# A graph kernel on one core: in-degrees from the sorted destinations, and the edge rows fetched in another block

## Chip, cores and metric

One core of one Trainium2 chip runs the whole kernel in one launch. The metric is the device time in microseconds. The engines are PE (TensorE; PEld is its weight load), DVE (VectorE), ACT (ScalarE), POOL (GpSimd) and SP (SyncE, which here only issues DMAs).

## What is computed

A stack of four graph layers on 3125 nodes with 16 features. The graph has 50000 random undirected edges, each in both directions, and a self-loop for each node: 103125 edges, sorted by destination. Each layer is x = x + layer(relu(layernorm(x))). Cut to what matters here:

```python
edge_index = stack([src, dst])                        # dst is sorted, 103125 edges, loops included
# layer 0, three GCN layers; adds its own self-loops once more
deg = segment_sum(ones, col);  norm = rsqrt(deg)[row] * rsqrt(deg)[col]
h = relu(agg(norm * (h @ W1)[row]) + b1); h = relu(agg(norm * (h @ W2)[row]) + b2); agg(norm * (h @ W3)[row]) + b3
# layer 1: messages of the sources summed per destination, between dense layers of 256
# layer 2: agg of x[src] * out_deg[src]**-0.5, times in_deg**-0.5 (degrees at least 1)
# layer 3: per edge, softmax over the in-edges of a destination, 16 x 16 channels:
e1 = (efeat @ W_msg + b_msg).reshape(E, 16, 16) * feat[src][:, :, None]
e2 = (efeat @ W_attn + b_attn).reshape(E, 16, 16) * feat[src][:, :, None]
ft = segment_sum(e1 * softmax_over_segment(e2, dst), dst).sum(axis=1)
```

## The kernel before

The kernel is a row of blocks. All five engines have a program in a block, and the next block begins when all of them are through, so nothing overlaps from one block to the next. The first blocks are these.

`build_edges`, first block (L203 to L318), the preparation. The edge table `edges` is a dense matrix of edge counts, sources in tiles of 128 partitions (25 tiles), destinations in 3136 columns, in bfloat16. It is built in strips of 16 destination columns from groups of 256 sorted edges; a "pair" is one group with one strip. The preparation finds group and strip of each of 600 pairs from the last destination of each of 403 groups (`cuts`, `below`, `gidx`; L243 to L288), clears the table (POOL 12 tiles, L236; DVE 13 tiles, L289), writes the diagonal (L298), gathers sources and destinations of the pairs with ten indirect DMAs on POOL (L231), and turns them into `qT` and `loT` (L301 to L318).

`build_edges`, second block (L324 to L377), the edge loop: 15 turns of 40 pairs. For a pair DVE makes two one-hot tiles `q_hot` (L337) and, for each five pairs, one `lo_hot` (L333); PE multiplies them and adds the strip as it stands (L358, L362); ACT copies the sum back into the strip (L375). POOL and SP have nothing to do.

`degrees` (L380 to L432): `times_edges` (L639) multiplies a matrix of ones with the whole table, 175 matmuls; the column sums are turned by 50 small matmuls (L406) into `indeg` and `deg`. SP loads `x` there.

`edge_groups` (L478 to L614) sorts the edges of each node into groups of at most four (`SLOTS`). It computes from `indeg` the first edge of each of 28160 groups (`start`) and which of the four slots are empty (`missing`). Its histogram is a product of one-hot tiles, 25 of each kind (L577 to L579, L532). It writes `start_wide` to memory, waits for that, loads it again one group further on into `q_following` (L612), and compares (L597, L599).

`Fetch` (L435 to L475) fetches the rows of edge features in the order of the groups. A turn is an index copy on POOL (L451) and four gathers of 128 rows of 512 bytes (L456) into `got0` or `got1`, and SP stores the tile to `edges_order` (L469). There are 56 turns, in pairs; a turn waits until the tile of two turns ago has been gathered and stored. 46 turns run beside `layer0`, the other ten beside `layer1_nodes`, two in each of its five rounds.

`layer0` (L650 to L809) runs `times_edges` three times on PE (the second with two groups of weights, 350 matmuls, L645), with ACT taking each chunk out (L712), small products (L728, L738, L745, L749, L756) and DVE work in between. `layer1_nodes` (L812 to L951) runs the dense layers of layer 1 over five parts. `layer1_sum` (L954) is the first reader of `edges_order`. After that come `layer1_post`, `layer2` and the attention with its own 880 gathers (L1481).

Waits: `Line.then` and `Steps.then` let an engine wait for its own instruction; other waits are counts of semaphores.

## Time and profile before

| what | us |
|---|---|
| median of 3 runs (lowest, highest) | 3127.6 (3121.86, 3134.39) |
| span of the profiled execution | 3126.8 |
| PE, DVE, ACT, POOL busy | 2351.3, 2224.5, 1698.7, 1398.1 |
| preparation, 0 to 66.2 | 66.2 |
| edge loop, 66.2 to 470.3 | 404.1 |
| degree pass, 470.3 to 516.4 | 46.1 |
| edge groups, 516.4 to 551.0 | 34.6 |
| layer 0, 551.0 to 879.3 | 328.3 |
| nodes of layer 1, 879.3 to 1005.0 | 125.7 |

The profile is one execution, whose span agrees with the median of the runs. "Busy" counts instructions in work; "idle before" is the time an engine stood still ahead of an instruction, with what ended it, and "issue" there means that the profile shows nothing it waited for. "remote" is a releaser that the records don't name. A row of windows gives the stretch, its length, then busy us and (x instructions) of PE, PEld, DVE, ACT and POOL (or of those engines that a filter leaves), the granted clock, the DMA share and GB/s. A row of the page's part 5 gives count, busy us, mean ns of one, and the idle time before them. PEclk is the clock granted to TensorE as a share of 2.4 GHz. Ends of matmuls are modelled, and instructions on POOL are recorded roughly.

### The profile page before, as it was taken

The page shows a single profiled execution, that of the slowest core. Times are in us where ns is not written, and L with a number is a line of the kernel's source. Part 1 is how long each engine was busy: PE and PEld are TensorE (multiplying, and loading weights), DVE is VectorE, ACT ScalarE, POOL GpSimd, SP SyncE. Part 2 cuts the span into 40 slices and gives each one's busy share as a digit, 9 for nine tenths or more (in the row PEclk, how much of TensorE's full clock was granted, in tenths as well). Part 3 has the DMA queues.
Part 4 walks back from the last instruction along what each step waited for, and adds up shares of the span by engine and source line. Part 5 has one row for each costly group of instructions (what it writes and reads, how often), then busy time and mean ns, then how long its engine had stood idle before and what let it go on. Part 6 is the DMA issues. An engine that isn't in the chain of part 4 may idle for free. (4 is left out here: it accounts for less than half of the span.)

```text
span 3126.8 us, 38694 instructions
## 1 busy us (share of the span) xinstructions
PE 2351.3 (75%) x8098; PEld 1032.6 (33%) x8099; DVE 2224.5 (71%) x3656; ACT 1698.7 (54%) x6693; POOL 1398.1 (45%) x1220
## 2 busy tenths in 40 slices
PE   1888887656675998854788888888888888888840
PEld 1444443232453555331232223322232222322220
...
GB/s 17 0 0 0 0 0 6 85 87 88 52 62 171 150 149 146 73 19 17 64 67 72 63 80 67 63 72 76 70 65 72 63 80 67 63 72 68 70 47 89
DMA packets 122372, 201.38 MB, mean 64 GB/s; under 512 B 55271, under 2 KB 76664, under 8 KB 116448
## 3 DMA queue, kind: packets, MB, share of 16 engines
q1 hardware_dynamic: 84320, 170.52, 15.6%
...
q14 instruction: 21, 0.17, 0.0%
...
## 5 line engine op out<-in xcount | busy, mean ns | idle before, releaser
L1481 POOL DMA_INDIRECT hs<-h_table,gix x880 | 1103.8, 1254 | 451.2 <-issue 271.5
L1574 ACT ACTIVATE e<-wps,hs 128x32 f32<-128x32 f32 x5632 | 1029.8, 402 | 235.2 <-PE wps L1505 142.3
L1505 PE MATMUL wps<-w_edge,ef 18*128 18x512 f32 x1760 | 577.6, 707 | 316.1 <-ACT e L1574 135.1
L1527 PE MATMUL slot_sums<-e,ident 128*128 128x512 f32 x1408 | 761.3, 691 | 9.7 <-DVE e L1676 7.0
L1527 PEld LDWEIGHTS slot_sums<-e,ident 128*128 128x128 f32 x1408 | 296.6, 222 | 493.3 <-issue 464.3
L1505 PEld LDWEIGHTS wps<-w_edge,ef 18*128 18x128 f32 x1760 | 159.1, 200 | 691.5 <-ACT e L1574 274.8
L358 PE MATMUL acc<-q_hot,lo_hot 128*128 128x400 bf16 x1200 | 306.0, 337 | 48.7 <-DVE q_hot L337 46.8
L1611 DVE TENSOR_TENSOR e<-wps,hs 128x2048 f32<-128x2048 f32 x132 | 301.9, 2287 | 41.1 <-PE wps L1505 34.0
L375 ACT CAST edges<-acc 128x400 f32 x600 | 293.5, 492 | 59.0 <-PE acc L362 32.5
L337 DVE TENSOR_SCALAR q_hot<-qcol,qT 128x400 bf16<-128x400 bf16 x1200 | 293.9, 322 | 9.7 <-PE acc L362 9.5
L456 POOL DMA_INDIRECT got<-in_edge_rows,ix x224 | 224.9, 1004 | 100.7 <-issue 92.7
L645 PE MATMUL acc<-edges,parts 128*128 x875 | 201.6, 382 | 80.9 <-issue 31.9
L1658 DVE TENSOR_TENSOR e<-e,shifts 128x1024 f32<-128x1024 f32 x220 | 256.7, 1218 | 0.0
L1584 ACT ACTIVATE e<-e 128x1024 f32<-128x1024 f32 x220 | 241.7, 1108 | 26.4 <-issue 11.0
L1676 DVE TENSOR_TENSOR e<-e 128x1024 f32<-128x1024 f32 x220 | 253.5, 1220 | 0.0
L1035 PE MATMUL acc<-edges,msg_parts 128*128 (+1 forms) x1050 | 210.3, 355 | 25.3 <-DMA msg_parts<-msg 25.3
L362 PE MATMUL acc<-edges,ident_b 128*128 x600 | 202.9, 338 | 17.2 <-ACT edges L375 17.2
L514 POOL IOTA q_laneI<- 128x256 int32 x1 | 0.3, 341 | 470.7 <-ACTq L511 470.7
L712 ACT ACTIVATE agg<-acc 48x448 f32<-48x448 f32 (+1 forms) x21 | 11.3, 539 | 300.4 <-PE acc L645 148.1
L779 DVE TENSOR_TENSOR y<-small,deg 128x512 f32<-128x512 f32 (+1 forms) x8 | 4.6, 575 | 217.7 <-remote 204.8
L358 PEld LDWEIGHTS acc<-q_hot,lo_hot 128*128 128x128 bf16 x1200 | 130.5, 140 | 82.8 <-DVE q_hot L337 59.9
L645 PEld LDWEIGHTS acc<-edges,parts 128*128 128x128 bf16 x875 | 87.8, 103 | 192.7 <-issue 132.0
...
## 6 DMA issues: line engine op xcount, KB each, us to landing
...
hs<-h_table,gix POOLq DMA_INDIRECT x880
...
```

What stands on the lines that cost most here:

```text
L337: ins = nc.vector.tensor_scalar(q_hot[:, k % HOTS, s, :], qcol[:, :], qT[:, s, at], None, ALU.is_equal)
L358: nc.tensor.matmul(total, lo_hot[:, k // HOTS % 2, :, k % HOTS * 2 + s], q_hot[:, k % HOTS, s, :], start=(s == 0), stop=False)
L375: nc.scalar.copy(edges[:, :, bass.ds(s16, W)], acc[:, k % BANKS, 0:QW].rearrange("p (t w) -> p t w", w=W)).then_inc(taken, 1)
L645: ins = nc.tensor.matmul(out[:, bass.ds(n, 1), 0:CW], lhs(k), edges[:, k, bass.ds(n * CW, CW)], start=(g == 0 and k == 0), stop=(g == last ...
L1481: nc.gpsimd.indirect_dma_start(out=hs[u][:, s, :], out_offset=None, in_=d["h_table"], in_offset=bass.IndirectOffsetOnAxis(ap=gix[u][:, s:s ...
L1505: nc.tensor.matmul(wps[:, bank, :], ef[u][k:k + KM, g * P:(g + 1) * P], w[k:k + KM, :], start=True, stop=True).then_inc(a_mult, 1)
L1527: ins = nc.tensor.matmul(sums[:, g % 2, :], ident[:, :], e[u][:, g * SLOTS + c, :], start=(c == 0), stop=(c == SLOTS - 1))
L1574: ins = nc.scalar.mul(e[u][:, s, at], wps[:, bank, at], hs[u][:, s, f:f + 1])
L1584: nc.scalar.activation(e2, e2, ACT.Exp).then_inc(a_exp, 1)
L1611: nc.vector.tensor_tensor(e[u][:, s0:s1, :].rearrange("p s (i c) -> p (s i) c", c=2 * F), wps[:, 0:s1 - s0, :].rearrange("p s (i c) -> p ( ...
L1658: nc.vector.tensor_tensor(e2, e2, bc(shift(u, g), 1, SLOTS), ALU.subtract).then_inc(a_sub, 1)
L1676: ins = nc.vector.tensor_tensor(pair[:, :, 1, :], pair[:, :, 0, :], pair[:, :, 1, :], ALU.mult)
```

## The change

`degrees` is gone. The preparation becomes `prepare_pairs`, then comes `edge_groups`, then `fill_edges` (the edge loop). All edge rows are fetched in `fill_edges`; `layer0` and `layer1_nodes` lose the fetch.

- In-degrees: for each of 3125 nodes ACT counts in which group of 256 sorted destinations the first edge of this node lies (`coarse`, one activation with an accumulated output for each tile of 128 nodes), POOL gathers these groups of `dst` (25 indirect DMAs, two sets of five), and ACT counts inside them (`fine`). The rank of the next node (two small matmuls, `later` and `corner`) minus a node's own is its in-degree.
- Compare and reduction of the pair search become one DVE instruction with an accumulated output.
- POOL clears ten tiles of the table ahead of the gathers, DVE eight and three; the last four tiles hold the tiles of the preparation (`lent`) and are cleared on POOL in `edge_groups`, where ACT writes their part of the diagonal.
- `edge_groups` computes also the square roots and reciprocals for `deg`, keeps the one-hot tiles in a ring of ten (a wait of DVE for PE), and leaves the load of `q_following` and the computation of `missing` to `fill_edges`.

```diff
+LENT = 4
...
-            build_edges(nc, io, keep, d, sem)
-            degrees(nc, io, keep, d, sem)
-            with nc.sbuf_tensor("start", [P, GORDER], I32) as keep["start"]:
-                with ExitStack() as fetching:
-                    fetch = Fetch(nc, fetching, io, keep, d, sem)
-                    edge_groups(nc, io, keep, d, sem)
-                    layer0(nc, io, keep, d, sem, fetch)
-                    layer1_nodes(nc, io, keep, d, sem, fetch)
+            with ExitStack() as building:
+                pairs = pair_tiles(nc, building)
+                prepare_pairs(nc, io, keep, d, sem, pairs)
+                edge_groups(nc, io, keep, d, sem, pairs)
+                fill_edges(nc, io, keep, d, sem, pairs, Fetch(nc, building, io, pairs, d, sem))
+            layer0(nc, io, keep, d, sem)
+            layer1_nodes(nc, io, keep, d, sem)
             layer1_sum(nc, io, keep, d, sem)
...
+    loT, qT, lane, qcol, strip, ident_b = (pairs[n] for n in ("loT", "qT", "lane", "qcol", "strip", "ident_b"))
+    BLANK = TILES * 10 // 25
+    MORE = BLANK + TILES * 8 // 25
...
+                nc.gpsimd.affine_select(out=ident[:, :], in_=ident[:, :], compare_op=ALU.not_equal, fill=1.0,
+                                        base=0, pattern=[[-1, P]], channel_multiplier=1).then_inc(b_consts, 1)
+                nc.gpsimd.affine_select(out=later[:, :], in_=later[:, :], compare_op=ALU.not_equal, fill=1.0,
+                                        base=-1, pattern=[[-1, P]], channel_multiplier=1)
+                nc.gpsimd.affine_select(out=corner[:, :], in_=corner[:, :], compare_op=ALU.not_equal, fill=1.0,
+                                        base=P - 1, pattern=[[-1, P]], channel_multiplier=1).then_inc(b_consts, 1)
+                nc.gpsimd.memset(edges[:, 0:BLANK, :].rearrange("p t c -> p (t c)").bitcast(I32), 0
+                                 ).then_inc(b_blank, 1)
+                pool.wait_ge(b_pairs, 1)
+                for k in range(PAIR_TILES):
+                    for rows_of, name in ((srcg, "src"), (dstg, "dst")):
+                        nc.gpsimd.indirect_dma_start(
+                            out=rows_of[:, k, :], out_offset=None,
+                            in_=io[name].rearrange("(g e) -> g e", e=GROUP),
+                            in_offset=bass.IndirectOffsetOnAxis(ap=gidxI[:, k:k + 1], axis=0),
+                        ).then_inc(b_gather, 16)
+                pool.wait_ge(b_groups, 1)
+                for t in range(TILES):
+                    r = t // SET
+                    if r >= 2 and t % SET == 0:
+                        pool.wait_ge(b_fine, (r - 1) * SET)
+                    nc.gpsimd.indirect_dma_start(
+                        out=rows[:, r % 2, t % SET, :], out_offset=None,
+                        in_=io["dst"].rearrange("(g e) -> g e", e=GROUP),
+                        in_offset=bass.IndirectOffsetOnAxis(ap=coarseI[:, t:t + 1], axis=0),
+                    ).then_inc(b_rows[r % 2], 16)
+
...
+                    ins.then_inc(b_pe, 1)
+                pe.wait_ge(b_rank, 1)
+                nc.tensor.matmul(after[:, :], later[:, :], rank[:, 0:TILES], start=True, stop=False)
+                nc.tensor.matmul(after[:, :], corner[:, :], rank[:, 1:TILES + 1], start=False, stop=True
+                                 ).then_inc(b_after, 1)
...
+                act.wait_ge(b_node, 1)
+                act.wait_ge(b_last, 1)
+                for t in range(TILES):
+                    if t >= 2:
+                        act.wait_ge(b_coarse, t - 1)
+                    nc.scalar.activation(sign[:, t % 2, :], last[:, :], ACT.Sign, bias=half_less[:, t:t + 1],
+                                         accum_out=coarse[:, t:t + 1]).then_inc(b_coarse, 1)
+                act.wait_ge(b_coarse, TILES)
+                for t in range(TILES):
+                    r = t // SET
+                    if t % SET == 0:
+                        act.wait_ge(b_rows[r % 2], 16 * SET * (r // 2 + 1))
+                    if t >= 2:
+                        act.wait_ge(b_fine, t - 1)
+                    nc.scalar.activation(sign[:, t % 2, 0:GROUP], rows[:, r % 2, t % SET, :], ACT.Sign,
+                                         bias=half_less[:, t:t + 1], accum_out=fine[:, t:t + 1]).then_inc(b_fine, 1)
+
...
+                v.add(nc.vector.tensor_copy(qcol[:, :], qcolI[:, :]))
+                dve.wait_ge(b_pe, 1)
+                for k in range(PAIR_TILES):
+                    v.then(nc.vector.tensor_scalar(below[:, :], cuts[:, :], pair[:, k:k + 1], 0.0, ALU.is_le, ALU.add,
+                                                   accum_out=gidx[:, k:k + 1]))
+                v.then(nc.vector.tensor_scalar(below[:, :], cuts[:, :], float(RUN), 0.0, ALU.is_le, ALU.add,
+                                               accum_out=middle[:, :]))
+                v.then(nc.vector.tensor_scalar(middle[:, :], middle[:, :], -1.0, float(RUN), ALU.mult, ALU.add))
...
+                nc.vector.tensor_scalar(first[:, :], first[:, :], float(W), None, ALU.mult).then_inc(b_pairs, 1)
+                v.add(nc.vector.memset(edges[:, BLANK:MORE, :], 0.0))
+
+                dve.wait_ge(b_coarse, TILES)
+                v.then(nc.vector.tensor_scalar(coarse[:, :], coarse[:, :], -0.5, 0.5 * GROUPS, ALU.mult, ALU.add))
+                v.then(nc.vector.tensor_scalar(coarse[:, :], coarse[:, :], float(GROUPS - 1), None, ALU.min))
+                nc.vector.tensor_copy(coarseI[:, :], coarse[:, :]).then_inc(b_groups, 1)
+                v.add(nc.vector.memset(rank[:, TILES:TILES + 1], float(EPAD)))
+                v.add(nc.vector.memset(edges[:, MORE:TILES - LENT, :], 0.0))
...
+                for t in range(TILES - LENT):
+                    w = min(P, COLS - t * P)
+                    v.add(nc.vector.tensor_copy(edges[:, t, t * P:t * P + w], ident[:, 0:w]))
...
+                v.then(nc.vector.tensor_scalar(fine[:, :], fine[:, :], -0.5, 0.5 * GROUP, ALU.mult, ALU.add))
+                nc.vector.scalar_tensor_tensor(rank[:, 0:TILES], coarse[:, :], float(GROUP), fine[:, :],
+                                               ALU.mult, ALU.add).then_inc(b_rank, 1)
+                dve.wait_ge(b_rank, 1)
+                dve.wait_ge(b_after, 1)
+                v.then(nc.vector.tensor_tensor(indeg[:, :], after[:, :], rank[:, 0:TILES], ALU.subtract))
+
+
...
+def fill_edges(nc, io, keep, d, sem, pairs, fetch):
...
+            @block.sync
+            def _(sp):
+                sp.dma_start(following[:, :], d["start_wide"][1:GTOTAL + 1].rearrange("(p g) -> p g", p=P)
+                             ).then_inc(q_short, 16)
+                with sp.Fori(0, fetch.PAIRS) as i:
+                    for v in range(2):
+                        fetch.store(sp, i, v)
+                fetch.wait_stored(sp, fetch.PAIRS)
+
+            @block.gpsimd
+            def _(pool):
+                for v in range(2):
+                    fetch.gather(pool, 0, v)
+                with pool.Fori(1, fetch.PAIRS) as i:
+                    for v in range(2):
+                        fetch.gather_again(pool, i, v)
+
...
 
+                v = Line(dve, q_missing)
+                dve.wait_ge(q_short, 16)
+                v.then(nc.vector.tensor_tensor(following[:, :], following[:, :], run[:, 1, :], ALU.subtract))
+                for c in range(1, SLOTS):
+                    v.then(nc.vector.tensor_scalar(missing[:, 0:GSTEPS, c], following[:, :], float(c), None, ALU.is_le))
                 dve.wait_ge(taken, RUNS + TURNS * BODY)
...
-def degrees(nc, io, keep, d, sem):
...
+def edge_groups(nc, io, keep, d, sem, pairs):
...
+                nc.gpsimd.memset(edges[:, TILES - LENT:TILES, :].rearrange("p t c -> p (t c)").bitcast(I32), 0
+                                 ).then_inc(q_blank, 1)
 
...
+                v.then(nc.vector.tensor_scalar(raw[:, 1, :], indeg[:, :], 1.0, None, ALU.max))
+                nc.vector.tensor_scalar(raw[:, 0, :], indeg[:, :], 1.0, 1.0, ALU.add, ALU.max).then_inc(q_raw, 1)
...
+                    nc.vector.tensor_scalar(lo_hot[:, at, 0, :], lane[:, 0:GSTEPS], lo[:, t:t + 1], None, ALU.is_equal)
+                    nc.vector.tensor_scalar(lo_hot[:, at, 1, :], lane[:, 0:GSTEPS], lo[:, t:t + 1], short[:, t:t + 1],
                                             ALU.is_equal, ALU.mult).then_inc(q_hot, 1)
-                dve.wait_ge(q_hist, 1)
+                v.wait_all()
+                dve.wait_ge(q_sqrt, 1)
+                v.add(nc.vector.reciprocal(deg[:, 0, :], raw[:, 0, :]))
+                v.add(nc.vector.reciprocal(deg[:, 2, :], raw[:, 1, :]))
+                dve.wait_ge(q_hist, TILES)
                 for a in range(2):
                     v.then(nc.vector.tensor_tensor_scan(run[:, a, :], zero[:, :], hist[:, a, :], 0.0,
                                                         ALU.add, ALU.add))
...
+                dve.wait_ge(q_done, 1)
+
+            @block.scalar
+            def _(act):
+                act.wait_ge(q_raw, 1)
+                nc.scalar.activation(raw[:, :, :], raw[:, :, :], ACT.Sqrt).then_inc(q_sqrt, 1)
+                act.wait_ge(q_blank, 1)
+                for t in range(TILES - LENT, TILES):
+                    w = min(P, COLS - t * P)
+                    ins = nc.scalar.copy(edges[:, t, t * P:t * P + w], ident[:, 0:w])
+                ins.then_inc(q_loops, 1)
+                act.wait_ge(q_sqrt, 1)
+                act.wait_ge(q_loops, 1)
...
                              ).then_inc(q_out, 16)
                 sp.wait_ge(q_out, 80)
-                sp.dma_start(following[:, :], d["start_wide"][1:GTOTAL + 1].rearrange("(p g) -> p g", p=P)
-                             ).then_inc(q_out, 16)
-                sp.wait_ge(q_out, 96)
...
-def layer0(nc, io, keep, d, sem, fetch):
+def layer0(nc, io, keep, d, sem):
...
                                  ).then_inc(c_w, 16)
-                with sp.Fori(0, FETCH0) as i:
-                    for v in range(2):
-                        fetch.store(sp, i, v)
                 sp.wait_ge(c_w, 16 * 12)
-                fetch.wait_stored(sp, FETCH0)
-
-            @block.gpsimd
-            def _(pool):
-                for v in range(2):
-                    fetch.gather(pool, 0, v)
-                with pool.Fori(1, FETCH0) as i:
-                    for v in range(2):
-                        fetch.gather_again(pool, i, v)
 
...
-def layer1_nodes(nc, io, keep, d, sem, fetch):
+def layer1_nodes(nc, io, keep, d, sem):
...
                                      parts[:, :, :, f * P:(f + 1) * P]).then_inc(n_dm, 16)
-                    for v in range(2):
-                        fetch.store(sp, FETCH0 + c, v)
                 sp.wait_ge(n_dh, 16 * ROUNDS)
                 sp.wait_ge(n_dm, 32 * ROUNDS)
-                fetch.wait_stored(sp, fetch.PAIRS)
-
-            @block.gpsimd
-            def _(pool):
-                for c in range(ROUNDS):
-                    for v in range(2):
-                        fetch.gather_again(pool, FETCH0 + c, v)
 
```

## Rows read from the trace of the kernel before

**Rows 1.** Windows of the first five stages and of the attention.
```profile
0.00:66.20 66.20, 6.24 (x22) 4.64 (x23) 47.65 (x81) 0.02 (x1) 27.99 (x22) 1.00 0.17 20
66.20:470.30 404.10, 336.93 (x1800) 188.21 (x1800) 375.94 (x1322) 312.78 (x615) 0.00 (x0) 1.00 0.00 0
470.30:516.40 46.10, 42.85 (x225) 25.43 (x225) 5.59 (x15) 1.53 (x2) 0.00 (x0) 0.89 0.05 5
516.40:551.00 34.60, 15.33 (x31) 4.04 (x31) 25.14 (x114) 0.00 (x0) 1.57 (x8) 0.50 0.03 10
551.00:879.30 328.30, 216.42 (x925) 114.66 (x925) 42.64 (x70) 11.54 (x22) 189.07 (x229) 0.74 0.27 74
...
1388.00:2950.00 1562.00, 1269.69 (x3072) 438.30 (x3072) 1410.12 (x1572) 1267.18 (x5825) 1103.76 (x880) 0.80 0.22 66
```

**Rows 2.** Timeline of the preparation: start us, us, engine, instruction, [idle before].
```profile
7.57 0.64 DVE L271 TENSOR_SCALAR below<-cuts,pair 128x403 f32<-128x403 f32 x1 [1.80 <-PE cuts L243]
8.24 0.57 DVE L272 TENSOR_REDUCE gidx<-below 128x1 f32<-128x403 f32 x1
...
17.20 0.17 DVE L288 TENSOR_SCALAR first<-first 128x5 f32<-128x5 f32 x1
...
21.58 17.13 DVE L289 MEMSET edges<- 128x20488 uint32 x1 [4.21 <-issue]
...
29.07 0.94 POOL L231 DMA_INDIRECT dstg<-in_dst,gidxI  x1 [0.30 <-issue]
30.01 15.88 POOL L236 MEMSET edges<- 128x18912 int32 x1
```

**Rows 3.** The page's part 5, ACT's copy out of PSUM in the edge loop.
```profile
L375 ACT CAST edges<-acc 128x400 f32 x600 | 293.5, 492 | 59.0 <-PE acc L362 32.5
```

**Rows 4.** Timeline at the end of the edge groups, SP's queue.
```profile
546.17 0.35 SPq L612 DMA_DIRECT2D q_following<-start_wide  x1
```

**Rows 5.** Windows of L645 alone, layer 0's three passes.
```profile
561.90:636.50 74.60, 49.61 (x175) 17.86 (x175) 0.75 0.34 91
668.00:778.30 110.30, 80.66 (x350) 34.38 (x350) 0.89 0.32 87
832.60:868.60 36.00, 35.75 (x175) 17.76 (x175) 0.93 0.00 0
```

**Rows 6.** Timeline behind the first pass, PE and DVE.
```profile
636.87 3.64 PE L728 MATMUL small<-w,agg 48*128 48x64 f32 x16 [9.55 <-issue]
...
643.50 0.69 DVE L779 TENSOR_TENSOR y<-small,deg 128x512 f32<-128x512 f32 x1 [81.92 <-remote]
```

**Rows 7.** The page's part 5, all gathers of edge rows on POOL.
```profile
L456 POOL DMA_INDIRECT got<-in_edge_rows,ix x224 | 224.9, 1004 | 100.7 <-issue 92.7
```

**Rows 8.** Timeline, POOL beside DVE, layer 0 and layer 1's nodes.
```profile
650.51 0.97 POOL L456 DMA_INDIRECT got<-in_edge_rows,ix  x1 [0.81 <-issue]
650.59 0.43 DVE L783 TENSOR_SCALAR y<-y 128x512 f32<-128x512 f32 x1
...
884.63 5.10 DVE L933 TENSOR_TENSOR edges<-edges,ident 128x128 bf16<-128x128 bf16 x25
...
885.77 0.22 POOL L451 COPY ix<-start 128x4 int32<-128x4 int32 x1
886.80 3.77 POOL L456 DMA_INDIRECT got<-in_edge_rows,ix  x1 [0.81 <-issue]
```

**Rows 9.** Timeline of DVE in the edge loop, one stretch of five pairs.
```profile
104.58 0.82 DVE L333 TENSOR_TENSOR lo_hot<-lane,loT 128x1280 bf16<-128x1280 bf16 x1
105.31 2.42 DVE L337 TENSOR_SCALAR q_hot<-qcol,qT 128x400 bf16<-128x400 bf16 x10
```

**Rows 10.** Windows of L1574 alone (ACT), attention's start and later.
```profile
1419.30:1442.40 23.10, 4.88 (x17) 0.50 0.07 6
...
1580.00:1700.00 120.00, 81.87 (x438) 0.82 0.24 73
```

381 lines of the change are left out of this document (172 added, 209 removed).

## The prediction, made before the changed kernel was run

> **What bounds the kernel now.** Read first by stage. The chain of work that ended last is of no help: it covers only the last steps. The windows [rows 1] are of more use: the code is a row of blocks that wait for one another, so each block's length is its own critical path, and what leaves a block leaves the time. The first five are the preparation of the pairs (66.2 us), the edge loop (404.1), the degree pass (46.1), the edge groups (34.6) and layer 0 (328.3); the nodes of layer 1 follow. Nothing behind those is changed, and no edge row is read before they end. In the edge loop DVE is busy 376 of 404 us and POOL not at all; in layer 0 it is the other way round. The second view is L645, the product with the edge table, pass by pass [rows 5]. The third pass of layer 0, with no fetch beside it, took 36.0 us for 175 matmuls. The first, with gathers beside it, took 74.6 us for the same 175, and the second 110.3 for 350. So the fetch is not free where it stands. The third view is the gathers on POOL and what DVE does to them [rows 7, 8].
>
> **Part 1: no degree pass, another way to the in-degrees.** Old way, three blocks ahead of layer 0 besides the loop: 66.2 + 46.1 + 34.6 = 146.9 us [rows 1]. The 46.1 go whole. In their place the preparation grows. DVE: six pairs of compare (0.64) and reduction (0.57) [rows 2] become six single instructions of about 0.67, so the pair indices come some 3.5 us earlier than 17.4, less about 1.2 for the node numbers and the ends: near 15. ACT: 25 activations over 403 columns, not in the trace; the nearest row is 0.49 for 400 columns out of PSUM [rows 3], and I take 0.6 for the accumulated output (bounds 0.49 to 0.8). From about 7 us they end near 22 (19 to 27), under DVE's clearing of eight tiles (8/13 of 17.1 us [rows 2], to 26); they cost nothing while that lasts. POOL is the path. Its clearing of ten tiles is 10/12 of 15.9 us = 13.2, now ahead of the gathers, so it ends near 17.5; then come ten gathers every 1.25 us (0.94 and a gap of 0.30 [rows 2]), to 30; then 25 new gathers of dst rows, 25 x 1.25 = 31.3, to 61. Beside them DVE runs its copies and its casts of 1280 columns, which hold gathers up (part 4): 0 to 12 us, I take 5. Landing, the last five activations, the two small matmuls and the subtraction: 5 to 10, I take 8. Sum 74 (66 to 83). DVE's own way (to 26, three tiles more 4, then what now lies between the end of POOL's clearing, 30.0 + 15.9, and 66.2, copies and casts, 20) ends near 50 and is hidden. The edge groups lose their tail, since the load of q_following is issued at 546.2, where 80 counts of q_out are there [rows 4], and the block ends at 551.0: 34.6 - 4.8 + 0.7 for two reciprocals = 30.5. Its ring of ten hot tiles asks DVE to wait for PE five tiles back, and PE kept up (bounds 0 and 2). The clearing of the four lent tiles (5.3 us on POOL) and four copies on ACT lie beside some 30 us of DVE work. New: 74 + 30.5 = 104.5. Change **-42** (-52 to -32).
>
> **Part 2: layer 0 without the fetch.** First pass 74.6 - 36.0 = 38.6; second 110.3 - 2 x 36.0 = 38.3 [rows 5]. Behind the first pass DVE starts on a finished small product 3.0 us late [rows 6]: 636.9 + 3.6 = 640.5, start 643.5. Together **-80**. The third pass begins at a lower clock, so twice its length is rather long for the second, and I take 87 as the upper bound; the lower is 0, if the stalls have another cause (a rival). The clock does not make the difference: it was 0.75 and 0.89 in the slow passes and 0.93 in the quiet one [rows 5], and there are gaps in which PE had nothing issued. SP's queue in that block loses 46 stores; the weight loads ahead of them are unchanged.
>
> **Part 3: nodes of layer 1.** Rounds there are a chain over PE, ACT and DVE; the last edge store only ends the block beside the last message stores. **-1** (-3 to 0).
>
> **Part 4: the fetch beside the edge loop.** Unhindered it is 224.9 + 100.7 = 325.6 us of POOL [rows 7], against 404.1 us of loop, so there are 78 us to spare. What does DVE's stream do to it? If the gather gets in at the next instruction's end, the mean wait is 3/4 x 0.12 + 1/4 x 0.41 = 0.19 us; 224 gathers and 56 index copies make 53 us. 326 + 53 = 379 < 404: hidden, with 25 us left. The bounds are 0 and, if it is starved through whole stretches, +148 (rival A). I take the fair case, because the index copy beside the same stream took 0.22 us, so a stream as such does not shut POOL out, and because DVE idles 28 us in the loop, where any gather gets in. The stores on SP have no queue behind them that anybody waits for; `missing` is computed behind the loop, where DVE waits for ACT's last copy: +2 (0 to 3). If the loop should become shorter than 379 us, this cover is gone and each microsecond of the rest is paid in full.
>
> Here the Trainium skill speaks against the change. Its page "SBUF — State Buffer", section "Who interferes with whom", says that a VectorE instruction in a two-port mode holds the port pair it shares with GpSimd for its whole length, and that descriptors of a DMA issued by GpSimd can't be written meanwhile. The 0.97 us gather with the fast tensor_scalar inside it does not agree for the part behind the start; the held-up gather agrees for the start.
>
> **Sum.** The profiled execution: 3126.8 (its span; the median of the runs is 3127.6, so the two are the same for this). 3126.8 - 42 - 80 - 1 + 2 = **3005 us**.
>
> **Rivals.**
> A. DVE starves the gathers. By the strict form a gather moves on only outside q_hot, that is 0.89 of every 3.31 us, so one gather in 3.3: 404/3.3 = 122 of 224 are done at the loop's end, and 102 x 1.45 (325.6/224) = 148 us stand bare: 3153. If one in three waits about 3 us, as one of the POOL instructions in the stream of 25 did, the mean is 2.7 us, 150 are done, 74 x 1.45 = 107: 3112. For: DVE works 93% of the loop, its instructions overlap. Against: the gather with the fast instruction inside. The page above would give the strict form.
> B. Slower: the stall moves along. With gathers at full pace PE had one matmul in 0.43 us in the first pass instead of 0.21 (74.6 and 36.0 over 175), and ACT, at the start of the attention, 17 short activations in 23.1 us, 1.36 us each, where later it had 438 in 120 [rows 10]. The loop needs one activation and three matmuls for a pair in 404.1/600 = 0.67 us. At 1.36 us a pair the 326 us of fetch cover 240 pairs, the other 360 take 242: the loop becomes 568, +164, and 3005 + 164 = **3169**. It decides (slower than 3142) from a mean of 1.16 us a pair during the fetch. For: it was seen twice. Against: both times DVE was idle, and in the attention as a whole, with DVE busy 1410 of 1562 us and 880 gathers on POOL [rows 1], ACT's pace is whole; in the loop DVE is busy and breaks up the gathers' rhythm. Once DVE waits for a stalled PE, though, it no longer breaks it up, so the state could hold itself.
> C. The change doesn't bring what it says in layer 0: the stalls of L645 belong to the code and not to the gathers. 3005 + 80 = 3085. Against: the same function ran the third pass and the degree pass (46.1 us with everything) without them.
>
> **Chances.** Forecast (2982 to 3035) 0.52; A 0.24 (3035 to 3153, likeliest 3112); B 0.17 (3090 to 3180, likeliest 3169); C 0.07. 0.5% is 15.6 us, about what a measurement of this kernel can tell from no change. Slower by more needs over 3142: most of B and a quarter of A, 0.18. Within: between 3111 and 3142, less what lies below: 0.06. Faster 0.76. Range 2982 to 3145: it leaves out B's upper part, a bit of A, and a preparation better than reckoned.
>
> **What would show it.** Right: L231's successor gathers end near 61 us, the block near 74, the loop starts near 105; the loop's block is 404 to 410 us, with POOL's last gather before its end and L337's successor at 0.24 us each; the three passes of layer 0 at 36, 70 and 36 us, that block at 248. A: POOL gathers far beyond 1 us while DVE keeps its pace, and a stretch behind the loop with POOL alone. B: PE and ACT idle for "issue" in the loop, POOL at 0.94, and the loop quick again once the fetch ends. C: passes unchanged with POOL empty. Wrong altogether if the 25 rank gathers are slowed so that the preparation passes 90 us.

## The result, and the profile after

The changed kernel took 3185.7 us (median of four runs), the kernel before 3126.5 beside it: a ratio of 1.0188 (1.0154 to 1.0223), slower by 1.9% where 3.9% less was forecast. The profiled execution has a span of 3170.7 us. It can be read by stages like [rows 1]. The windows of the changed kernel, with the columns of [rows 1], in order the preparation, the edge groups, the edge loop with the fetch, and layer 0:

```profile
0.00:85.80 85.80, 8.60 (x28) 6.18 (x29) 55.63 (x87) 28.71 (x102) 56.16 (x52) 0.90 0.26 56
85.80:120.40 34.60, 15.34 (x31) 4.04 (x31) 29.21 (x114) 2.26 (x6) 6.70 (x8) 0.50 0.02 7
120.40:689.00 568.60, 402.26 (x1800) 201.38 (x1800) 392.70 (x1325) 292.97 (x600) 239.37 (x280) 0.81 0.19 52
689.00:925.50 236.50, 185.58 (x925) 111.12 (x925) 42.61 (x71) 11.56 (x22) 0.00 (x0) 0.79 0.00 1
```

| stage | before | forecast | after |
|---|---|---|---|
| preparation | 66.2 | 74 | 85.8 |
| degree pass | 46.1 | 0 | 0 |
| edge groups | 34.6 | 30.5 | 34.6 |
| edge loop | 404.1 | 406.1 | 568.6 |
| layer 0 | 328.3 | 248.3 | 236.5 |
| all behind it | 2247.5 | 2246.5 | 2245.2 |
| span | 3126.8 | 3005 | 3170.7 |

The degree pass, layer 0 and all behind it came out as forecast or better. The preparation and the edge groups together are 15.9 us over the forecast (120.4 against 104.5). The loss is the edge loop, +164.5 us. Three groups of the changed kernel, answering to [rows 3] and [rows 7] (busy time, mean ns, then the idle time before them and what ended it):

```profile
L505 ACT CAST edges<-acc 128x400 f32 x600 | 293.0, 493 | 300.0 <-PE acc L492 137.3 <-remote 98.3 <-issue 45.9
L462 DVE TENSOR_SCALAR q_hot<-qcol,qT 128x400 bf16<-128x400 bf16 x1200 | 307.4, 327 | 113.3 <-remote 60.7 <-PE acc L492 45.5 <-issue 6.9
L531 POOL DMA_INDIRECT got<-in_edge_rows,ix x224 | 227.4, 1015 | 98.4 <-issue 96.4 <-POOL ix L526 1.6 <-DMA edges_order<-got 0.3
```

The gathers are as quick as in [rows 7] (1015 ns, 98.4 us of gaps): DVE did not starve them. ACT does its 600 copies in the old time for each, but idles 300 us around them (30 of these ahead of the first). 98 us end with "remote" and some with "issue", for which the profile shows no releaser in the kernel. I read the waits for PE as the same stall seen from behind PE; the profile doesn't show that by itself. Windows of L505 alone, the first while the fetch runs and the second behind it:

```profile
121.00:463.00 342.00, 120.15 (x249) 0.69 0.32 86
463.00:687.00 224.00, 172.82 (x351) 1.00 0.00 1
```

That is 342/249 = 1.37 us a pair beside the gathers and 224/351 = 0.64 behind them. Rival B had said 1.36 us a pair and a loop of 568 us. The 1.37 is a mean over an uneven stretch: between 250 and 300 us there were 25 copies, between 300 and 350 us 60.

### The profile page after: what moved, and what is told of

Same layout as the page of the kernel before. It is cut to its first block and busy times, and to the rows that moved or that the text cites. A ratio compares the mean times of both kernels' runs of the same rounds, so it can differ in the third digit from the quotient of the medians.

```text
span 3170.7 us, 38247 instructions
## 1 busy us (share of the span) xinstructions
PE 2347.7 (74%) x7879; PEld 1019.1 (32%) x7880; DVE 2247.7 (71%) x3651; ACT 1712.2 (54%) x6783; POOL 1434.8 (45%) x1251
## 5 line engine op out<-in xcount | busy, mean ns | idle before, releaser
L505 ACT CAST edges<-acc 128x400 f32 x600 | 293.0, 493 | 300.0 <-PE acc L492 137.3
L462 DVE TENSOR_SCALAR q_hot<-qcol,qT 128x400 bf16<-128x400 bf16 x1200 | 307.4, 327 | 113.3 <-remote 60.7
L488 PE MATMUL acc<-q_hot,lo_hot 128*128 128x400 bf16 x1200 | 346.3, 374 | 54.1 <-DVE q_hot L462 47.1
L492 PE MATMUL acc<-edges,ident_b 128*128 x600 | 223.2, 372 | 115.3 <-issue 78.7
L531 POOL DMA_INDIRECT got<-in_edge_rows,ix x224 | 227.4, 1015 | 98.4 <-issue 96.4
L737 PE MATMUL acc<-edges,parts 128*128 x875 | 174.1, 364 | 40.5 <-DVE mean L849 13.5
L488 PEld LDWEIGHTS acc<-q_hot,lo_hot 128*128 128x128 bf16 x1200 | 141.1, 143 | 104.5 <-DVE q_hot L462 59.9
L1702 DVE TENSOR_TENSOR pairs<-e 128x1536 f32<-128x1536 f32 x88 | 131.0, 1489 | 30.0 <-ACT e L1645 30.0
L1133 ACT COPY efT<-tr 128x512 f32<-128x512 f32 x56 | 32.8, 586 | 215.7 <-PE tr L1115 215.7
L492 PEld LDWEIGHTS acc<-edges,ident_b 128*128 128x128 bf16 x600 | 60.3, 100 | 265.5 <-issue 261.7
```

What stands on the lines that cost most here:

```text
L462: ins = nc.vector.tensor_scalar(q_hot[:, k % HOTS, s, :], qcol[:, :], qT[:, s, at], None, ALU.is_equal)
L488: nc.tensor.matmul(total, lo_hot[:, k // HOTS % 2, :, k % HOTS * 2 + s], q_hot[:, k % HOTS, s, :], start=(s == 0), stop=False)
L492: nc.tensor.matmul(total, ident_b[:, :], edges[:, :, bass.ds(s16, W)], start=False, stop=True).then_inc(multiplied, 1)
L505: nc.scalar.copy(edges[:, :, bass.ds(s16, W)], acc[:, k % BANKS, 0:QW].rearrange("p (t w) -> p t w", w=W)).then_inc(taken, 1)
```

## A condition that comes and goes

All experiments were measured on other occasions, and the kernel before was quicker on all of them, by nearly 4% on five of eight. This has to be told first, since every reading depends on it. The first line is the measurement of the result; each other line is one session, all on one chip. Numbers with a star come from a single run:

| kernel before, us | with it (ratio to it) |
|---|---|
| 3126.5 | the changed kernel 1.0188 |
| 3011.7 | e1 0.985, e2 0.997\*, e3 0.976, e4 0.969\* |
| 3009.1 | the changed kernel (e5) 0.979, the kernel before again (e6) 1.001\*, e7 0.975 |
| 3008.1 | e8 0.969 |
| 3012.7, chip A | e9 1.006\*, e10 0.9945 |
| 3068.5\* | e11 1.011\* |
| 3073.2, chip A | e12 0.983, e13 0.9825 |
| 3118.1, chip A | the changed kernel (e14) 1.0134, e15 0.990 |
| 3011.1 | e16 0.967, e18 0.993, e17 0.9685 |

I call some 3010 us the quiet condition and anything above 3060 the stalled one. Chip A had both, so it is no fixed property of a chip. Nothing in the kernels differs between them. A ratio is only ever taken within one session.

The two conditions also differ in what the traces hold, and this bears on every reading below. A trace records the updates of semaphores. All thirteen traces of the quiet condition hold 30.5 to 31.2 thousand such records, all seven of the stalled one (before, after, e11 to e15) 19.0 to 20.8 thousand, with the same number of instructions in the same kernel. The missing ones lie where gathers run: of the landings of DMAs, before and e6 (the same kernel, quiet) have 173 and 180 in the preparation, but 1222 and 3864 in layer 0 and 8704 and 15736 in the attention. Beside the edge loop the 224 gathers should leave 3584 records of landing and the 56 stores 896. e5 (the changed kernel, quiet) has 3498 and 878 of them, the profile of the result 776 and 187. So a wait that ends with "remote" or "issue" in a stalled stretch may only lack the record of its releaser, and these words don't say what the engines waited for. And as every time here is that of an execution with such a record, no run shows whether the stall is there without the recording.

## Experiments

**The fetch alone put back** (e1: the in-degrees stay new, the fetch goes back into layer 0, 46 turns, and the nodes of layer 1, ten; the expectation calls the 46 "pairs of turns", they are turns).

```diff
-                fill_edges(nc, io, keep, d, sem, pairs, Fetch(nc, building, io, pairs, d, sem))
-            layer0(nc, io, keep, d, sem)
...
+                fill_edges(nc, io, keep, d, sem, pairs)
+            layer0(nc, io, keep, d, sem, fetch)
...
```

> The changed kernel with the fetch alone put back where it was (46 pairs of turns in layer 0, five in the nodes of layer 1); the new in-degrees stay. It splits the two halves of the change. Theory: the edge loop's 570 us are all due to the fetch beside it and layer 0's gain is all due to the fetch leaving. Then the fill is back at 404 to 408 us, layer 0 at 328, the preparation and edge groups stay at 85.4 and 34.9, and the time is 3126.8 + 19.2 - 46.1 + 0.3 = 3100 us (3095 to 3110). Rival (the fill is slow through something else that the change moved, such as the memory in which the pair tiles now lie or the missing counts behind the loop): the fill stays above 450 us and the time above 3150.

Measured: 2966.9 us, a ratio of 0.9854 (0.9838 to 0.9871). Windows of the loop and of layer 0:

```profile
119.00:508.00 389.00, 338.20 (x1800) 188.89 (x1800) 373.80 (x1325) 295.42 (x600) 0.18 (x1) 1.00 0.00 0
508.00:787.00 279.00, 186.51 (x925) 111.35 (x925) 43.59 (x72) 11.56 (x22) 191.30 (x230) 0.75 0.31 87
```

The loop without the fetch is not 404 but 389 us: 15 us that nothing in the forecast explains (e10 does). Layer 0 with its 46 turns of the fetch is 279 us, not 328. In the quiet condition the fetch in layer 0 does not stall PE (e6 below has the passes); POOL's own length bounds the block.

**Gathers first, stores behind** (e2). SP's stores wait for all gathers, and POOL no longer waits for stores, so what is stored are the rows of the last turns.

```diff
+                for v in range(2):
+                    sp.wait_ge(fetch.gathered[v], 16 * TURN * fetch.PAIRS)
...
-        pool.wait_ge(self.stored[v], i * 16)
```

> In the changed kernel all 224 gathers run first, each turn waiting for the gathers only, and all 56 stores follow when they are done, still beside the edge loop; so the rows stored are those of the last turns, and the edge features are not the reference's. It tells gathers from stores. Theory G, the software gathers stall PE, ACT and DVE: a pair takes about 1.4 us while POOL gathers (some 330 us, 235 pairs) and 0.65 us beside the stores, fill some 560 to 570 us. Theory S, the stores' traffic on SP does it: 0.67 us a pair while POOL gathers, over 1 us beside the stores, fill some 430 to 480 us.

Neither theory was tested: in the quiet condition the loop took 394.5 us with the gathers beside it, 0.66 us a pair. (The gathers and stores then ran some 79 us past the loop.)

**Paced gathers** (e3), each turn waiting for ten pairs more.

```diff
+                        pool.wait_ge(taken, i * 20 + 10 * v)
```

> The changed kernel with each turn of four gathers also waiting until ACT has taken out ten pairs more, so that 56 turns spread over 560 of the 600 pairs. A turn takes POOL about 6.0 us, ten pairs 6.5 to 6.7. Theory U, the stall needs some 20 us of unbroken gathers and a pause of POOL of about 2 us ends it: as soon as pairs slow down POOL waits, so the stall can't hold itself; fill 405 to 460 us, time 3010 to 3065. Theory V, the stall is there from the first gathers on and lasts as long as they are issued: in each turn 6.0 us pass at 1.4 us a pair, the other 6 pairs take 4 us, 10 us a turn, fill about 570 us and the time as the changed kernel's, 3160 to 3190.

Measured: 2934.1 us, 0.976 (0.973 to 0.979), fill 397.9 us. There was no stall to be held off, so theories U and V stay undecided. It says that a fetch stretched over the whole loop costs 9 us above the bare 389.

**ACT clears in POOL's place** (e4), in the preparation and in the edge groups. DVE's 21 copies of the diagonal also move behind its transposed copies.

```diff
-                nc.gpsimd.memset(edges[:, 0:BLANK, :].rearrange("p t c -> p (t c)").bitcast(I32), 0
-                                 ).then_inc(b_blank, 1)
+                for t in range(BLANK):          # on ACT, behind the 25 coarse activations
+                    words = edges[:, t, :].bitcast(F32)
+                    nc.scalar.copy(words, nought[:, 0:1].broadcast_to(list(words.shape))).then_inc(b_blank, 1)
...
```

> The changed kernel with POOL's two clearings (10 tiles in the preparation, 4 in the edge groups) done by ACT as copies of a zero, the 21 diagonal copies on DVE moved behind the transposed copies. Theory L: POOL's clearing shuts out DVE's small instructions for its whole length (13.4 us of DVE L334 in the preparation, 5.4 us of DVE L627 in the edge groups, both ending with a POOL memset). Then both are under 0.3 us, the pair indices are ready near 15 us instead of 27, the ten gathers end near 28, the preparation is 72 to 80 us instead of 85.4 and the edge groups 29 to 31 instead of 34.9. Rival W, these instructions wait for something else: they stay long, the preparation stays over 83 us.

Lines of the changed kernel's timeline, the preparation and the edge groups (start, length):

```profile
3.56 13.36 DVE L334 CAST own<-turnI 128x5 f32<-128x5 int32 x1
3.66 13.23 POOL L265 MEMSET edges<- 128x15760 int32 x1
...
87.22 5.35 POOL L599 MEMSET edges<- 128x6304 int32 x1
87.23 5.38 DVE L627 TENSOR_SCALAR raw<-indeg 128x25 f32<-128x25 f32 x1
```

The same two DVE instructions in e4's, and its windows of the two stages:

```profile
3.58 0.18 DVE L337 CAST own<-turnI 128x5 f32<-128x5 int32 x1
...
71.19 0.17 DVE L628 TENSOR_SCALAR raw<-indeg 128x25 f32<-128x25 f32 x1
```

```profile
0.00:69.80 69.80, 7.88 (x28) 5.63 (x29) 42.54 (x87) 42.75 (x112) 40.11 (x52) 0.86 0.32 69
69.80:100.30 30.50, 15.32 (x31) 4.03 (x31) 24.09 (x114) 7.98 (x10) 1.57 (x8) 0.50 0.02 8
```

Theory L holds. A cast of five columns on DVE took 13.36 us while POOL was clearing, and 0.18 us without that. The preparation went to 69.8 us (82.6 in e5, the changed kernel in the same condition), even below the 72 expected, the groups from 34.7 to 30.5, the forecast's own number. How much of the preparation's 12.8 us is due to the moved diagonal copies isn't separated; the two DVE instructions alone give 13.2 and 5.2.

**The changed kernel and the kernel before again** (e5 and e6, both unaltered).

> The changed kernel itself, unaltered, beside the kernel before, timed again and with a profile of its own. In the experiments so far the kernel before took 3011.7 us instead of 3126.5, and no run stalled beside gathers, so this asks whether the stall belongs to the kernel or to where it ran. If the kernel before is at about 3012 again: the changed kernel has no stalls either, its edge loop is about 395 to 408 us and its time that of the quick-preparation kernel (2919) plus 16 + 5 = 2935 to 2945, a ratio of 0.975 to 0.978. If the kernel before is at about 3127: the changed kernel is at 3172 to 3200 with a loop of 567 us, a ratio of 1.015 to 1.022. A mixture, such as 3012 beside 3180, would make the stall a thing of the changed kernel alone.

> The kernel before, unaltered, for a profile beside the others. If it is at about 3012: the passes of the product with the edge table in layer 0 are about 36, 70 and 36 us instead of 74.6, 110.3 and 36.0, though the fetch is beside them, layer 0 is bound by POOL's gathers and takes 280 us instead of 328, the edge loop is still 404 us with 15 loads of ACT's table, one in each turn of 40 pairs, and the other 65 us are in the attention. If it is at about 3127, all is as in the profile shown.

In the same session 2940.5 against 3009.1 us, a ratio of 0.979 (0.975 to 0.983): the changed kernel is 2.1% faster in the quiet condition and 1.3 to 1.9% slower in the stalled one. First e5's windows of loop and layer 0, and two groups of it; then e6's window of layer 0:

```profile
117.30:528.00 410.70, 344.23 (x1800) 191.58 (x1800) 383.75 (x1325) 295.22 (x600) 301.91 (x280) 0.97 0.27 72
528.00:764.50 236.50, 185.82 (x925) 112.29 (x925) 42.44 (x70) 11.54 (x22) 0.00 (x0) 0.79 0.00 1
```

```profile
L505 ACT CAST edges<-acc 128x400 f32 x600 | 295.2, 492 | 130.3 <-PE acc L492 105.1
L531 POOL DMA_INDIRECT got<-in_edge_rows,ix x224 | 284.9, 1272 | 98.2 <-issue 50.6 <-POOL ix L526 45.2 <-DMA edges_order<-got 2.4
```

```profile
551.00:832.00 281.00, 185.53 (x925) 111.11 (x925) 43.12 (x71) 11.55 (x22) 191.28 (x230) 0.74 0.31 87
```

Of ACT's idle time 105.1 of 130.3 us end with PE now, and the gathers are slower instead: 1272 ns, since DVE keeps its pace. Layer 0 of the kernel before is 281.0 us where it was 328.3 [rows 1]. The rest of the difference of 118 us between the conditions is nearly all in the attention: from its start to the end of the span 1747.3 us in the profile shown and 1680.3 in e6, 67 us.

The quiet ledger, e6 to e5: preparation +16.4 (66.2 to 82.6), degree pass -45.7, groups -0.1, fill +6.4 (404.3 to 410.7), layer 0 -44.5 (281.0 to 236.5), the rest -3.0; together -70.5.

**Quick preparation with paced gathers** (e7), e3 and e4 together.

> The changed kernel with both trials together: ACT clears in POOL's place, and each turn of four gathers waits for ten more pairs. If the kernel before is at about 3012: preparation 66 to 70, edge groups 27, edge loop 398 with nothing behind it, 2926 - 18 = 2908 us (2903 to 2915), 0.966 of the kernel before. If it is at about 3127, theory U (the stall needs unbroken gathers) gives a loop of 405 to 460 us and a ratio of 0.96 to 0.98, theory V (the stall is there whenever gathers run) a loop of about 560 us and a ratio of 1.01.

Measured 2931.8 us (0.975), not 2908: this time the paced fetch ended late and the fill took 416 us. Pacing adds to the fetch's length what a turn loses when it starts late, and never gets it back.

**The last two of 28 fetch pairs in layer 0** (e8, and again as e17; both on e4's kernel).

```diff
+FETCH0 = GORDER // TURN // 2 - 2
...
-                with pool.Fori(1, fetch.PAIRS) as i:
+                with pool.Fori(1, FETCH0) as i:
...
```

> The quick-preparation kernel, with only 26 of the 28 pairs of fetch turns beside the edge loop and the last two pairs (16 gathers) at the start of layer 0, where POOL is idle. Where the kernel before takes 3010 us: the fetch of 28 pairs took 400 us beside a loop of 396 to 400 (gathers of 1.27 us instead of 1.00 beside DVE's stream) and the block ended 8 to 10 us behind the loop's last instruction; 26 pairs need 371 us, so the loop alone ends the block, 396 to 398 us, and layer 0 stays at 238: 2919 - 9 = 2910 us (2905 to 2916), 0.966 to 0.969 of the kernel before. Rival: the fetch slows the loop itself as much as before and layer 0 pays for the two pairs, then 2916 to 2925. Where the kernel before takes 3127 the stall is back: the ratio is 1.00 to 1.02.

> The split kernel without rests (26 pairs beside the loop, two in layer 0), a second time: 0.969 where the kernel before takes 3010; where it takes 3073 to 3127 the loop stalls as the changed kernel's, 480 to 560 us, and the ratio is that of the changed kernel less 0.010: 0.99 to 1.005. The long rests should beat it there by 0.01 to 0.02.

2915.7 us, 0.9694 (0.968 to 0.971), and 2912.9 us, 0.9685 (0.966 to 0.971). The fill is 395.6 us; without the split it was 406.7 (e4). The end of the fetch no longer sticks out behind the loop.

**What holds a gather up** (e9): q_hot's source at every other element, so that DVE leaves its fast form.

```diff
...
-                            ins = nc.vector.tensor_scalar(q_hot[:, k % HOTS, s, :], qcol[:, :], qT[:, s, at], None,
+                            ins = nc.vector.tensor_scalar(q_hot[:, k % HOTS, s, :], qcol[:, :, 0], qT[:, s, at], None,
```

> The changed kernel with the column numbers that DVE compares in the q_hot instructions held at every other element, so that these leave the two-times-fast form (0.24 us for 400 columns) and take about 0.42 us; it tells what holds up the gathers beside the loop (1.27 us mean beside it, 1.00 without; a tenth of them 2.7 us, as long as a run of ten q_hot). Theory P, fast instructions back to back keep the port from POOL: the gathers are at 1.0 us mean, none over 1.7, and all 224 end 340 us after the first, while the loop takes about 600 us. Rival Q, any DVE instruction does it: gathers of 4 us and more appear, mean 1.4 us or more. If the kernel before takes 3127 here, the stall is back and PE, ACT and DVE show it beside the gathers: then a loop with more slack (1.0 us a pair by DVE) still falls to 1.4 us a pair.

A stretch of e5's timeline, and then e9's groups:

```profile
299.88 2.77 POOL L531 DMA_INDIRECT got<-in_edge_rows,ix  x1 [0.30 <-issue]
300.11 2.41 DVE L462 TENSOR_SCALAR q_hot<-qcol,qT 128x400 bf16<-128x400 bf16 x10
...
302.95 1.13 POOL L531 DMA_INDIRECT got<-in_edge_rows,ix  x1 [0.30 <-issue]
```

```profile
L462 DVE TENSOR_SCALAR q_hot<-qcol,qT 128x400 bf16<-128x400 bf16 x1200 | 416.0, 426 | 0.0
...
L531 POOL DMA_INDIRECT got<-in_edge_rows,ix x224 | 236.3, 1055 | 98.3 <-issue 52.4 <-POOL ix L526 45.2 <-DMA edges_order<-got 0.6
```

In e5 a gather that meets the head of ten q_hot back to back ends 0.13 us behind the tenth; 23 of the 224 took over 2.5 us. In e9 DVE is busier (495.8 of 497.7 us of the block) and the gathers take 1055 ns, 223 of 224 under 1.13 us. So the fast form of these tensor_scalars holds the gathers up, not DVE's load; theory P. It is shown for tensor_scalar only: the stream in [rows 8] that held a gather for 3.77 us was of tensor_tensor. The loop's 600 us were wrong, it took 497.7: the slow form costs 0.35 us of busy time apiece.

**One ACT instruction ahead of the loop of the kernel before** (e10).

```diff
+                nc.scalar.copy(warm[:, :], ones[:, 0:1])
                 act.sem_inc(taken, RUNS)
```

> The kernel before with one copy of a 128x1 column on ACT ahead of the edge loop and nothing else. The profile of before has 15 loads of ACT's table, 1.28 us each, one in each turn of 40 pairs of the edge loop; the changed kernels have none there, and with no fetch beside it their loop took 388 us instead of 404. Theory M: the loads come because nothing on ACT ran ahead of the loop, and they cost the loop those 16 us. Then they are gone but one, the loop is 388 us, and the time is 16 us under the kernel before, a ratio of 0.9945 (0.993 to 0.996). Rival: the 16 us come from the shorter preparation or from where the pair tiles lie; then the loop stays at 404 and the ratio at 1.000.

ACT in the edge loop of the kernel before, a row that the forecast had not read, and then of e10:

```profile
L375 ACT ACT_TABLE_LOAD x15 | 19.2, 1283 | 96.9 <-PE acc L362 96.9
```

```profile
L368 ACT ACT_TABLE_LOAD x1 | 1.3, 1283 | 66.3 <-PEq L203 66.3
```

Ratio 0.9945 (0.9925 to 0.9966), loop 388.0 us instead of 404. With no ACT instruction ahead of the loop, its table is loaded anew in each of the 15 turns. The change got these 16 us as a side effect; its Sign activations on ACT stand ahead of the loop.

**Five kinds of fetch in one loop** (e11).

```diff
+                Q = fetch.PAIRS // 4              # POOL; a loop of Q pairs of turns for each kind
...
+                fetch.wait_stored(pool, Q)
+                with pool.Fori(Q, 2 * Q) as i:
+                    for v in range(2):
+                        pool.wait_ge(fetch.gathered[v], i * (16 * TURN))
+                        fetch.gather(pool, i, v)
+                fetch.wait_stored(pool, 2 * Q)
...
```

> The changed kernel with the fetch beside the edge loop cut into five stretches, so that one run tells what stalls PE and ACT, if anything does: (1) 14 turns of gathers with their stores, as in the changed kernel, (2) 14 turns of gathers with no store, (3) the 14 stores of these, one behind the other, POOL waiting (they store what the two buffers hold then, so these edge rows are not the reference's), (4) 14 turns with stores, POOL resting before every second turn until everything of the turn before has landed and is stored, some 5 us, (5) 14 turns as in (1). Where the kernel before takes about 3010 us, as in all experiments so far: 0.65 to 0.68 us a pair in all five, the fill 400 to 415 us. Where it takes about 3127: theory G (gathers stall the engines): about 1.4 us a pair in 1, 2 and 5, and 0.67 in 3; theory S (the stores' traffic): slow in 1, 3 and 5, quick in 2; theory U (20 us of unbroken gathers are needed): quick in 4 too; theory V (whenever gathers run): in 4 in between, about 1.1.

The kernel before took 3068.5 us, a stalled condition at last. Windows of ACT's copies (their count is that of the pairs): the start and the end of stretch 1, then 2 in three parts, 3, 4, the start of 5 and the rest of it, and the loop with no fetch:

```profile
118.00:178.00 60.00, 38.85 (x81) 0.96 0.27 75
178.00:207.00 29.00, 12.77 (x27) 0.79 0.32 88
213.00:228.00 15.00, 8.99 (x19) 1.00 0.13 31
228.00:258.00 30.00, 15.76 (x33) 0.94 0.19 44
258.00:298.00 40.00, 13.69 (x29) 0.68 0.19 45
300.00:332.00 32.00, 22.48 (x47) 0.90 0.31 115
332.00:448.00 116.00, 77.29 (x159) 1.00 0.19 54
448.00:458.00 10.00, 6.30 (x13) 1.00 0.28 72
458.00:538.00 80.00, 23.83 (x50) 0.58 0.33 90
538.00:618.00 80.00, 60.78 (x124) 0.99 0.06 6
```

Us a pair: 0.74 and 1.07 in stretch 1, 0.79, 0.91 and 1.38 in 2, 0.68 in 3, 0.73 in 4, 0.77 and 1.60 in 5, 0.65 with nothing. Stretch 2 has gathers and no store, and stalls; stretch 3 has stores at 115 GB/s and no gather, and doesn't. Theory G holds and S falls, in this one run. The records of landing go the same way: stretch 2 has 228 of its 896, stretch 3 all 224. Whether it is the issuing on POOL or the landing of the rows that does it, the run doesn't tell, since a gather has both. In 4 the same gathers with rests of 4 us cost little. The stall sets in some tens of us after the last rest (about 60, 45 and 15 us in the three unbroken stretches), so theory U holds in kind, but the delay is not a fixed number.

**Rests in the whole fetch** (e12, rests of 4 us, and again as e18; e13, rests of 2 us; all on e4's kernel). 22 pairs of turns run beside the loop and six in layer 0, in e13 24 and four.

```diff
+    def rest(self, pool, i):
+        pool.wait_ge(self.stored[1], i * 16)      # e13: self.gathered[1], i * (16 * TURN)
...
```

> The quick-preparation kernel with a rest of POOL before every second turn until the turn before is stored (4 us), 22 of 28 pairs of turns beside the edge loop, six in layer 0. A pair of turns takes 11.8 us, 2 us of hold-ups and 4.1 us of rest, 18 us: 22 take 396 us, six 108 in layer 0 of 238. Where the kernel before takes 3010 us: loop 396 to 402, layer 0 238 to 242, time 2912 to 2925. Where it takes 3068 to 3127: theory U (the stall needs a longer unbroken stretch than 12 us): the loop is at 400 to 410 all the same, layer 0 at 240 to 250, and the gain on the kernel before is 90 + 16 to 60 us, a ratio of 0.955 to 0.97. If the rests don't hold the stall off in the end, the loop is at 480 us and more and the ratio above 0.985.

> The same with shorter rests, only until the last gather of the turn before has landed (some 2 us instead of 4), 24 pairs beside the loop and four in layer 0: 24 x 15.9 = 382 us. Where the kernel before takes 3010 us: as with the long rests, 2910 to 2922. Where it takes 3068 to 3127: if 2 us are enough, as one pause of 2.2 us seemed to be in layer 0 of the kernel before, the loop is at 400 to 410; if they are not, the loop falls to 1.0 us a pair or slower in parts and ends after 450 to 560 us, and the ratio lies 0.015 or more above that of the long rests.

> The kernel with rests of 4 us in all of the fetch, 22 pairs beside the loop and six in layer 0, a second time: 0.983 where the kernel before takes 3073 (loop 453 us), 0.97 where it takes 3010, and, if the stall grows as in the changed kernel, 0.985 to 0.995 where it takes 3118.

With the kernel before at 3073.2: 0.983 (0.980 to 0.986) and 0.9825 (0.974 to 0.991). Fill blocks 454.1 and 452.1 us, 0.75 us a pair: the worst is gone, but not all of the stall. Long and short rests can't be told apart. With the kernel before at 3011.1 the long rests gave 0.993, not 0.97. There DVE holds up the gathers (1421 ns mean in e18), 22 pairs took 460 us instead of 396, and the block waited 67 us for them. So rests in all of the fetch are a loss where there is no stall.

**The changed kernel a third time, and the fetch back with the quick preparation** (e14, unaltered; e15, e4's kernel with the edit of e1).

> The changed kernel, unaltered, a third time. Where the kernel before takes about 3010 us: 2940 as in the second time, ratio 0.979, loop 400 us. Where it takes about 3070: half of the stall, loop 480 to 520 us, ratio 0.995 to 1.01. Where it takes about 3127: loop 567 us, ratio 1.015 to 1.022. The more the kernel before is stalled, the worse the ratio, since the fetch stands beside 600 pairs that need three engines in turn, where in the kernel before it stands beside two passes that need PE.

> The quick-preparation kernel with the whole fetch back in layer 0 and the nodes of layer 1, as in the kernel before. Its ratio should not depend on the stall much, since both kernels have the fetch in the same place: shorter by 147 - 97 = 50 us of preparation and groups and by 16 us of ACT's table, so 3010 - 61 to 66 = 2944 to 2950, ratio 0.979 to 0.980, or 3070 - 66 = 3004, 0.979, or 3127 - 66 = 3061, 0.979. If it is far from 0.979 where the stall is there, the stall depends on more than the place of the fetch.

Kernel before at 3118.1. The changed kernel: 1.0134 (1.009 to 1.017). Windows of loop and layer 0, first of e14, then of e15:

```profile
118.70:671.00 552.30, 406.29 (x1800) 204.37 (x1800) 398.70 (x1325) 292.34 (x600) 239.91 (x280) 0.83 0.20 53
671.00:907.50 236.50, 186.71 (x925) 112.39 (x925) 42.13 (x70) 11.56 (x22) 0.00 (x0) 0.79 0.00 1
```

```profile
100.50:490.50 390.00, 339.69 (x1800) 189.47 (x1800) 373.98 (x1325) 295.43 (x600) 0.18 (x1) 0.98 0.00 0
490.50:843.00 352.50, 225.84 (x925) 114.31 (x925) 42.85 (x71) 11.56 (x22) 190.02 (x230) 0.70 0.25 69
```

The stall is thus reproduced, on a chip that had been quiet. These two traces are the plainest comparison of all, both from one stalled session. (They differ in the preparation too, which matters little to the loop: 406.7 us in e4 and 410.7 in e5.) The edge loop takes 552.3 us with the fetch beside it and 390.0 without, so the fetch costs it 162.3 us. Layer 0 takes 236.5 us without the fetch and 352.5 with 46 turns of it, 116.0 more. The ten turns in the nodes of layer 1 cost nothing that shows (2240.7 us behind layer 0 in e15, 2242.3 in e14). In this condition the same fetch thus costs 46 us more beside the loop than where it stood. e15 is at 0.990 (0.987 to 0.993), worse than the 0.979 expected. I have no profile of the kernel before from that session, so whether its layer 0 was stalled as long is not known.

**Half of the fetch in each stage, thinned** (e16, on e4's kernel): 14 pairs beside the loop, one for every 42 pairs of it, and 14 with rests in layer 0.

```diff
...
+                    pool.wait_ge(taken, i * 42)
+                    fetch.rest(pool, i)
...
```

> The quick-preparation kernel with half of the fetch (14 pairs of turns) beside the edge loop, one pair for every 42 pairs of the loop, so 12 us of gathers and 16 us of rest, and the other half in layer 0 with rests of 4 us (14 x 17 = 238 us). Theory U: the gathers' bursts are short and the rests long, so no stall in the loop: 392 to 410 us, and layer 0 at 240 to 260; ratio 0.965 to 0.972 in any condition. If the stall depends on the share of time with gathers only in proportion (theory V), about half of the loop's loss stays: loop 460 to 480, ratio near 0.99 where the kernel before takes 3118.

2910.4 us, 0.9668 (0.965 to 0.969), fill 393.0 and layer 0 238.0 us. It beats both kernels in the quiet condition, level with e8 and e17. The condition was quiet again, so whether it would also beat them in the stalled one is not shown.

## Why the prediction was wrong, step by step

**Part 4 failed, and it decides.** "Hidden, with 25 us left" was worked out for POOL alone. What was wrong was the other direction: what the fetch does to the loop. +164.5 us against +2, and as the loads of ACT's table fell away in the same block, the stall's own size is 568.6 - 389 = 180 us. e14 and e15 show the same in one session: 552.3 us with the fetch, 390.0 without. The stall was seen in [rows 5] and in [rows 10] and priced as rival B, to within a microsecond (568), in part by luck: its slow part was taken at 326 us and took 342, its quick part at 242 and took 224, and a second stalled measurement (e14) gave 552. The chance of 0.17 was too low. The argument against B, that a busy DVE breaks up the gathers' rhythm, is refuted: once PE stalls DVE idles (113 us), and the gathers run at full pace. The last sentence of B had named that. Part of the loss is the clock. The changed kernel's timeline, a matmul behind a gap and then a stretch where PE has no gap:

```profile
147.07 0.51 PE L492 MATMUL acc<-edges,ident_b 128*128 x1 [1.54 <-issue]
...
148.04 0.54 PE L492 MATMUL acc<-edges,ident_b 128*128 x1
...
148.37 0.87 PE L488 MATMUL acc<-q_hot,lo_hot 128*128 128x400 bf16 x2
...
149.04 0.54 PE L492 MATMUL acc<-edges,ident_b 128*128 x1
```

One pair takes 1.00 us there: PE at 1.2 GHz, the lower of its two levels, is alone slower than the loop, which runs at 0.64 us a pair at the upper one. The granted clock is 0.69 over the fetch, and here it is low behind a gap of PE. I take it that the stall's gaps bring a low clock, which makes the pairs slower still; how much of the 180 us it is, no run separates. It is not all of it: the slowest pairs took 1.6 us (e11), more than the 1.00 of PE alone.

**Part 4's own sum, where it can be seen.** In the quiet condition the gathers took 284.9 + 98.2 and the index copies 17.0 us, 400 in all, against the 379 forecast: held-up time 60 us on the gathers (284.9 - 224.9), where 53 were forecast, and the copies themselves were left out of the sum, only their waits were in it. The reading that a gather waits only for the running instruction was wrong: it can wait for all ten. Rival A's mild form is what happened there, at a tenth of its price: the block took 410.7 us, some 10 of them behind the loop's last instruction, until the last turn was stored. The Trainium skill, in "SBUF — State Buffer", section "Who interferes with whom", has one engine hold the shared pair "for the whole instruction" in DVE's two-port mode; e9 agrees that the form of the instruction decides (1055 ns against 1272), and e5 shows a wait over ten instructions in a row (2.77 us), which is longer than one.

**Part 1 was mis-sized.** 120.4 us against 104.5 for both stages. POOL's clearing was taken as 13.2 us of POOL beside DVE work; its length was right (13.23) and "beside" was wrong. It held DVE up for the same time, so that the pair indices came at 27 us and not at 15, and ACT's coarse activations began at 20.9 and not at 7. In the groups "5.3 us ... lie beside some 30 us of DVE work" failed in the same way, 5.4 us. e4 shows both by taking them away. The same section of the Trainium skill's page "SBUF — State Buffer" has it both ways: whoever of the two issues first keeps the pair, and the other "fully blocks". The forecast read it in one direction only, DVE against POOL. The trace agrees on the blocking (13.36 us); on the order it doesn't clearly, since by the profile's rough starts the cast began 0.10 us ahead of the clearing.

**Part 2 was right**, and better than sized: the passes of L737 took 35.1, 67.7 and 36.2 us, the block 236.5 against 248. But its -80 belongs to the stalled condition. In the quiet one the passes are whole even with the fetch (35.1, 67.7 and 36.1 in e6), POOL bounds the block, and the gain is 44.5. Rival C is out in both. **Part 3**: -2.3 against -1, all that lies behind layer 0 taken together.

**Not in the forecast at all**: the 15 table loads, -16 us (e10), with a row of their own in the trace of before.

The sum: 3005.4 (before it was rounded) + 11.8 (preparation) + 4.1 (groups) + 162.5 (loop) - 11.8 (layer 0) - 1.3 (the rest) = 3170.7, as measured.

**What stays open.** That the fetch beside the loop makes the stall is shown by taking it away; what makes the condition is not, since the same chip had 3012.7, 3073.2 and 3118.1 us for one kernel, and neither is why gathers stall PE, ACT and DVE under it. The trace has no releaser for it ("issue", "remote"), and most records of landing are missing just there. The recording itself is thus a rival that no run excludes: it may be slowed by the gathers and slow the engines in turn, or records and engines may suffer from one cause. Where the program's memory lies, or other load on the chip, was not varied either. That it goes by the gathers and not by the stores rests on one run (e11).
